# A grouped adapter kernel in float32r: half of each activation tile's low part is computed on GpSimd instead of VectorE

## The reference

```
y   = einsum('bsi,boi->bso', x, weight[ids])
h   = einsum('bsd,nrd->nbsr', y, lora_A)                        # 8 adapters, rank 16
out = x + einsum('bsd,od->bso', y, W) + bias
        + einsum('nbsr,nor->bso', h, lora_B * (32/16 * lora_weights))
```

## Time and profile before

| | |
|---|---|
| median of three runs | 1545.56 us (1544.95 to 1545.78) |
| the profiled execution | 1546.04 us |
| its span | 1543.9 us |
| TensorE busy | 1500.0 us, 97% |
| VectorE, ScalarE, GpSimd busy | 51%, 25%, 31% |

### The profile page before, as it was taken

One profiled execution on the slowest core, in us unless ns is written; L12 is line 12 of the kernel. 1 busy time (PEld: TensorE's weight loads), 2 busy tenths in 40 slices (PEclk: granted clock), 3 DMA queues, 4 the chain that ended last, 5 costly groups with the idle time before them and its releaser, 6 DMA issues.

```text
span 1543.9 us, 27859 instructions
## 1 busy us (share of the span) xinstructions
PE 1500.0 (97%) x6352; PEld 1200.4 (78%) x6353; DVE 790.3 (51%) x1183; ACT 386.6 (25%) x493; POOL 476.6 (31%) x644
## 2 busy tenths in 40 slices
PE   6889999999999999999799999999999999999998
PEld 3668888888888888888588888888888888888886
DVE  7767666766677567377773333333333333333330
ACT  3234333433344333344441010010101010010100
POOL 4723443334433433633311121212122121212121
PEclk9989999999999999999899999999999999999999
DMA  8887777877788686678865555555555555555553
GB/s 239 260 199 176 193 191 177 202 163 191 190 205 203 181 198 163 186 189 197 199 160 159 141 141 140 139 138 144 136 149 136 139 143 139 140 139 142 136 136 82
DMA packets 175345, 257.85 MB, mean 167 GB/s; under 512 B 22616, under 2 KB 131288, under 8 KB 175320
## 3 DMA queue, kind: packets, MB, share of 16 engines
q1 hardware_dynamic: 103464, 138.97, 37.8%
q10 hardware_dynamic: 51824, 73.48, 19.2%
q0 software_dynamic: 20032, 45.12, 10.1%
HBM read 181.99 MB, written 75.50 MB: 167 GB/s over the span
## 4 chain that ended last, share of the span: by engine, by line
PE 86%; DVE 3%; DMA 3%; issue 2%; ACT 2%; SPq 1%; ACTq 1%; DVEq 0%; POOLq 0%; POOL 0%
PE ps L703 29%; PE ps L704 29%; PE ps L705 29%; DMA w_raw<-in_L_cond_weight_dram 3%; DVE w_lo L564 1%; DVE w_turn L510 1%; SPq L199 1%; ACTq L421 1%; ACT stage L418 1%; SPq L221 1%; ACT w_hi L392 0%; DMA x_raw<-in_x_dram 0%; DVE x_turn L594 0%; ACT x_hi L400 0%; PE ps L685 0%
## 5 line engine op out<-in xcount | busy, mean ns | idle before, releaser
L703 PE MATMUL ps<-w_hi,x_hi 128*128 (+1 forms) x2096 | 833.9, 398 | 23.0 <-ACT stage L418 10.6
L704 PE MATMUL ps<-w_lo,x_hi 128*128 (+1 forms) x2096 | 832.9, 397 | 0.0
L705 PE MATMUL ps<-w_hi,x_lo 128*128 (+1 forms) x2096 | 832.6, 397 | 0.0
L703 PEld LDWEIGHTS ps<-w_hi,x_hi 128*128 128x128 f32 x2096 | 396.4, 189 | 121.4 <-issue 15.5
L705 PEld LDWEIGHTS ps<-w_hi,x_lo 128*128 128x128 f32 x2096 | 396.3, 189 | 95.7
L704 PEld LDWEIGHTS ps<-w_lo,x_hi 128*128 128x128 f32 x2096 | 396.4, 189 | 95.3
L199 POOL DMA_DIRECT2D x_raw<-in_x_dram x544 | 290.5, 534 | 436.7 <-DVE x_turn L594 291.0
L400 ACT ACTIVATE x_hi<-x_turn 128x512 fp32r<-128x512 f32 x272 | 160.5, 626 | 792.3 <-DVE x_turn L594 482.4
L373 POOL TENSOR_TENSOR stage<-stage,w_raw 128x1024 f32<-128x1024 f32 x64 | 154.2, 2409 | 595.3 <-DMA stage<-in_x_dram 595.3
L594 DVE STREAM_TRANSPOSE x_turn<-x_raw 128x256 f32<-128x256 f32 x544 | 193.6, 414 | 156.8 <-DMA x_raw<-in_x_dram 118.7
L601 DVE TENSOR_TENSOR x_lo<-x_turn,x_hi 128x512 fp32r<-128x512 f32 x272 | 185.2, 717 | 150.6 <-ACT x_hi L400 149.0
(11 more groups left out here) (64 smaller groups left out, 31.8 us busy)
## 6 DMA issues: line engine op xcount, KB each, us to landing
w_raw<-in_L_cond_weight_dram SPq DMA_DIRECT2D x248, 256.0 KB, 5.5
y_scr<-stage ACTq DMA_DIRECT2D x144, 256.0 KB, 4.1
x_raw<-in_x_dram POOLq DMA_DIRECT2D x544, 64.0 KB, 3.0
x_raw<-y_scr SPq DMA_DIRECT2D x128, 256.0 KB, 2.7
stage<-in_x_dram SPq DMA_DIRECT2D x128, 256.0 KB, 3.7
out_dram<-stage ACTq DMA_DIRECT2D x128, 256.0 KB, 2.9
base_sb<-in_L_ffn_W_dram POOLq DMA_DIRECT2D x8, 512.0 KB, 5.4
weff<-fold_sb POOLq DMA_DIRECT2D x8, 512.0 KB, 5.7
```

Source lines behind the costliest of these rows:

```text
L703: mm(ps[b][:, cols], x_hi[b][:, t, :], hi, start=t == 0, stop=False)
L704: mm(ps[b][:, cols], x_hi[b][:, t, :], lo, start=False, stop=False)
L705: last = mm(ps[b][:, cols], x_lo[b][:, t, :], hi, start=False, stop=t == KT - 1)
```

## The change

From tile 5 on (the sixth), and up to tile 71, GpSimd subtracts the second half of each tile (`x_lo[...][:, 4:8, :]`). Its order is: load tile n, then split tile n-2. VectorE subtracts only the first half of these tiles. Tiles 0 to 4, and the 64 tiles of the second stage, are split as before, both halves on VectorE. `x_ready` becomes two semaphores, one for each half, since two engines now raise them. TensorE waits for both, VectorE for the half that it overwrites. GpSimd's loop now goes over four tiles.

```diff
-        x_ready = sem("x_ready")
+        x_ready = [sem(f"x{h}_ready") for h in range(2)]
...
+            def split_x(n, b):
+                pool.wait_ge(x_rounded, 2 * n + 2)
+                nc.gpsimd.tensor_tensor(x_lo[b][:, KT // 2:, :], x_turn[1][:, :, :], x_hi[b][:, KT // 2:, :],
+                                        ALU.subtract).then_inc(x_ready[1], 1)
+
             load_x(RING + 1, 1)
-            with pool.Fori(3, SLOTS // 2) as g:
-                for b in range(2):
-                    load_x(2 * g + b, b)
+            for n in range(RING + 2, 2 * RING):
+                load_x(n, n % 2)
+                if n - 2 > RING:
+                    split_x(n - 2, (n - 2) % RING)
+            with pool.Fori(2, SLOTS // RING) as g:
+                for u in range(RING):
+                    load_x(g * RING + u, u % 2)
+                    split_x(g * RING + (u - 2), (u - 2) % RING)
+            for n in range(SLOTS - 2, SLOTS):
+                split_x(n, n % RING)
...
-                turn_x(n, b, raw)
+                turn_x(n, b, raw, loaded is x_loaded)
...
-            def turn_x(n, b, raw):
+            def turn_x(n, b, raw, shared=False):
                 for h in range(2):
                     if not (isinstance(n, int) and n == 0):
 
-                        dve.wait_ge(x_ready, 2 * n + (h - 1))
+                        dve.wait_ge(x_ready[h], n)
...
-                for h in range(2):
+                for h in range(1 if shared else 2):
                     dve.wait_ge(x_rounded, 2 * n + (h + 1))
                     ts = slice(h * KT // 2, (h + 1) * KT // 2)
-                    tt(x_lo[b][:, ts, :], x_turn[h][:, :, :], x_hi[b][:, ts, :], ALU.subtract).then_inc(x_ready, 1)
+                    tt(x_lo[b][:, ts, :], x_turn[h][:, :, :], x_hi[b][:, ts, :], ALU.subtract).then_inc(x_ready[h], 1)
...
-                pe.wait_ge(x_ready, 2 * slot + 2)
+                pe.wait_ge(x_ready[0], slot + 1)
+                pe.wait_ge(x_ready[1], slot + 1)
```

More of the change, by code:

```diff
@@ L707, in products @@
                     last.then_inc(tile_done, 1)
-            pe.wait_ge(x_ready, 2)
+            pe.wait_ge(x_ready[0], 1)
+            pe.wait_ge(x_ready[1], 1)
             pe.wait_ge(fold_moved, 2)
@@ L740, in _ @@
             for u in range(RING):
-                pe.wait_ge(x_ready, 2 * (SLOTS + u) + 2)
+                pe.wait_ge(x_ready[0], SLOTS + u + 1)
+                pe.wait_ge(x_ready[1], SLOTS + u + 1)
                 pe.wait_ge(moved, SLOTS - RING + u + 1)
@@ L746, in _ @@
                     t = g * RING + u
-                    pe.wait_ge(x_ready, 2 * t + (2 * SLOTS + 2))
+                    pe.wait_ge(x_ready[0], t + (SLOTS + 1))
+                    pe.wait_ge(x_ready[1], t + (SLOTS + 1))
                     pe.wait_ge(out_added, t - (RING - 1))
```

## The result

| | before | changed |
|---|---|---|
| median | 1545.55 us (4 runs) | 1648.67 us (4 runs, 1646.45 to 1652.34) |
| ratio | | 1.0669, interval 1.0653 to 1.0685 |
| span of the profiled execution | 1543.9 us | 1644.8 us |

The change makes the kernel 103 us slower.

A forecast was written before the change was run, and what follows sets the result against it. Preparation of weights and tiles, running close to TensorE's pace, was taken to bound stage one's end. Adding 98.8 us for stage one and 5.0 us at the restart gave 103.8 us more, 1649 us; range 1620 to 1692 us.

The forecast's parts named there:

- (1): VectorE loses one 128x512 subtraction on each of 67 tiles, worth 0.65 us apiece.
- (2): GpSimd gets that subtraction at an estimated 1.20 us, range 0.65 to 2.41 us.
- (3): In GpSimd's queue the split follows eight load issues, starting 6.2 us after the tile's turn and ending at 7.4 us.
- (4): VectorE's next second-half turn waits for GpSimd's split, GpSimd's next load for that turn: 8.20 us per tile, taken as 8.3.
- (5): Tile loads in stage one still land before VectorE needs them, so their landing stays hidden.
- The rank: One expert's weights plus n tiles take 25.7 + 8.3(n-1) us; stage one 758.2 against 659.4 us, +98.8 us.
- (6): TensorE restarts 32.6 us after the last expert's weights begin, before 27.6 us: +5.0 us; tile 71 tight but not late.
- (7): Costed at nothing: GpSimd's busy time, TensorE's second semaphore wait per tile, and the second stage.
- Rival B: Each rank's last GpSimd split also holds up a VectorE weight subtraction: up to 18 us more, 1667 us, chance 0.13.
- C: TensorE's lead of three tiles absorbs part of the delay: some 20 us less, 1629 us, chance 0.05.
- D: The split is hidden and VectorE relieved of 43 us of work, so the kernel is faster: 1533 us, chance 0.05.
- E: TensorE's 97% busy time is the true bound, so no difference: 1546 us, chance 0.02.

The follow-up runs named there:

- a ring without the hold: Changed kernel with GpSimd's split cut to one column at its place in the queue, VectorE doing both subtractions: 1606.49 us.
- the run with early indices: Kernel before the change, with both sample numbers of a tile read before GpSimd waits for the turned tile: 1544.41 us, ratio 0.9991.

## Why the prediction was right

The forecast was 1649 us, 103.8 us more for the profiled execution; the median is 1648.67 us, and the span grew by 100.9 us. By its steps:

(1) and (2), the prices. VectorE's single subtraction is 0.65 us, as said. GpSimd's is 1.30 us, not 1.20 us: half of the 128x1024 price and 0.1 us over.

(3) and (4), the ring. Said 8.20 us, with the loop's branch 8.3 us; the undisturbed step is 8.28 us. Its parts stand differently. From the end of the split to the next issue it is 1.49 us, where the sum had 0.1 + 0.72 + 0.70 = 1.52 us, and the split's 0.1 us more fill the rest. Three of the 51 steps of 15 ranks take 11.0 to 11.2 us: in two of them GpSimd waits 3.56 us between the halves of a load with nothing that the profile names, in the third its first issue comes 3.5 us after the turn. They bring the mean to 8.5 us; the sum had no such term.

(5), the landing stays hidden: right, VectorE's waits for tile loads in the whole stage fell from 118.7 us to 22.4 us. But for one of 4.0 us at the start, those left are before the first half of a tile whose second half then waits for GpSimd's split.

The rank: said 25.7 + 8.3(n-1). Measured for four tiles without a loop gap 49.6 us, said 50.6 us: the step from the last turn to the next weights is 1.2 us and not 1.85 us. The subtraction begins right at the end of the turn, and VectorE then idles 0.66 us, where the sum took the 1.1 us of the earlier trace rows; why it idles less isn't shown. The 14 ranks took 756.6 us, said 758.2 us. Two errors cancel here, shorter ends of ranks (0.7 us each, 9 us in all) and longer steps (0.2 us each, 10 us in all). That the sum came so close is in part luck; each part alone is right to 10 us.

(6), the restart: said 32.6 us after the last expert's weights, measured 32.3 us. Tile 71 was not late; there is no wait after the restart, and the second stage goes at 11.2 us a tile as before.

(7), costed at nothing: GpSimd's busy time grew by 88 us and none of it shows beyond the ring.

The weights, taken over at 22.4 us a rank, measured 22.3 us, and that is luck as well. Rival B was half right: its mechanism is there, 2.24 us for a subtraction of 1.2 us, but it doesn't come on top of 22.4 us. In a ring without the hold the stretch is 21.7 us, probably because the weights have more time to arrive in a longer rank, and about half of the hold comes on top of that. It cost some 8 us of the 103, by a comparison of runs that differ in more than the hold, and not 18 us. The Trainium skill says that a VectorE instruction with two SBUF inputs and a GpSimd one that reads SBUF keep each other off the shared port pair for the whole instruction (SBUF — State Buffer, on the shared port pair). The 3.89 us row agrees with that.

Rivals C, D and E fell: no delay was absorbed, and TensorE's 97% did not protect it. VectorE's freed work bought only the shorter ends of ranks, which the sum had in part. Of the 67 subtractions, 43 us, some 16 us came back as longer weight subtractions.

Of the signs, one was off in its make-up. TensorE was to wait some 100 us in all; its idle time grew by 75.6 us, and the other 25.3 us are products that took longer at the lower clock. The sum isn't touched, since it followed the preparation and not TensorE.

One sentence was too strong. "The preparation has 3.5 us to spare in such a rank" is right for the rank shown, but ranks of five took 49.4 to 51.3 us before, against 56 us of TensorE, and the run with early indices shows that such slack is cut off by the limit of three tiles and not used up evenly. The sum didn't rest on that sentence, as it added up the new ring from its own parts and compared two milestones.

## What to carry to other kernels

Before work is moved to an engine that "idles 70% of the time", follow whom the moved step frees, and what stands ahead of it in its new queue. Here a buffer's release was put behind eight DMA issues, and the next eight wait for the same buffer's next use. That ring of 8.3 us, of which only 1.3 us are arithmetic, set the stage; one more buffer gives back 85 us of the 103, the release issued first 78 us. An engine that shows 97% busy can still be the one that waits: add up the preparation of a unit (here a rank) and compare it with the time the busy engine takes for it. A saving counts only where such a sum exceeds it, as the same 0.7 us a tile was worth 36 us in one kernel and nothing measurable in the other.

## What the runs showed of the hardware

- A DMA issued on GpSimd for 32 partitions of 2x256 float32 takes 0.53 us there and lands after 3.0 us in the median (kernel before); one for all four groups of partitions takes 1.33 us and lands after 7.9 us (the same kernel with one DMA a sample). Merging four into one made the issues 1.8 times cheaper (2.36 to 1.33 us), while the landing came 4.9 us later.
- Such issues are not cheap on the other queues either: one sample in one DMA takes 1.09 us of ScalarE's queue (median), and two take 3.16 us from the start of the first to the end of the second. On SP a small one takes 0.56 us (median), and 18 took 19.05 us with what stood between them.
- A subtraction on VectorE with both inputs in SBUF waits out two GpSimd subtractions that begin 0.26 us after it (3.89 us for 1.23 us), while these keep their 1.3 us.
- GpSimd took 0.20 us for a one-column operation with two inputs, 1.30 us for 512 columns and 2.41 us for 1024.
